# Regrouping the routed experts' passes in the last batch of a fused gated mixture-of-experts kernel

## The reference, cut to what matters

```python
s0, s1, s2 = (_dense(h, share_wi[i], share_wo[i]) for i in range(3))
out_a = relu(h @ expert_wi[type_idx]) @ expert_wo[type_idx]
out_b = relu(h @ expert_wi[type_idx + 1]) @ expert_wo[type_idx + 1]
expert_out = out_a * wa + out_b * wb
gi = concatenate([expert_out[:, 0], s0[:, 0], s1[:, 0], s2[:, 0]], axis=-1)
g = softmax(relu(gi @ gate_w1) @ gate_w2, axis=-1)
out = expert_out * g0 + s0 * g1 + s1 * g2 + s2 * g3
```

## Time and profile before

| | |
|---|---|
| median of 3 runs | 1036.35 us |
| the profiled execution's own time | 1037.89 us |
| its span, first to last instruction | 1035.9 us |
| TensorE matmul busy | 1029.4 us (99%) |
| TensorE weight load busy | 853.9 us (82%) |
| VectorE busy | 806.9 us (78%) |
| ScalarE busy | 415.5 us (40%) |
| granted TensorE clock | 1.000 |

### The profile page before, as it was taken

The page is one execution under the profiler, slowest core; times in us unless marked ns, Lnnn a source line. Parts: engine busy times, 40 slices in busy tenths (PEclk is TensorE's granted clock), DMA queues, the critical chain, the costliest instruction groups (busy, mean ns, idle before and its releaser), DMA issues.

```text
span 1035.9 us, 12766 instructions
## 1 busy us (share of the span) xinstructions
PE 1029.4 (99%) x4784; PEld 853.9 (82%) x4784; DVE 806.9 (78%) x1369; ACT 415.5 (40%) x695; POOL 16.4 (2%) x26
## 2 busy tenths in 40 slices
PE   9999999999999999999999999999999999999998
PEld 6688888888888888888888888888888888888898
DVE  6989977799767988489785997659976699745236
ACT  7654455533344234422434233442333423333232
POOL 1200000000000000000000000000000000000000
PEclk9999999999999999999999999999999999999999
DMA  6388999786454754465544664546645475456581
GB/s 214 123 294 287 299 366 373 291 303 236 152 203 153 264 193 163 162 235 204 208 166 159 242 234 146 196 164 245 215 149 203 163 258 201 142 191 216 200 323 74
DMA packets 38304, 223.02 MB, mean 215 GB/s; under 512 B 4515, under 2 KB 5283, under 8 KB 16611
## 3 DMA queue, kind: packets, MB, share of 16 engines
q1 hardware_dynamic: 35938, 209.63, 56.9%
q0 software_dynamic: 2304, 12.58, 3.2%
HBM read 188.51 MB, written 33.69 MB: 215 GB/s over the span
## 4 chain that ended last, share of the span: by engine, by line
PE 95%; DMA 2%; DVE 2%; issue 0%; ACT 0%; SPq 0%; DVEq 0%
PE ps_up L680 14%; PE ps_up L710 14%; PE ps_up L711 14%; PE ps_down L752 14%; PE ps_down L753 14%; PE ps_down L756 14%; PE ps_aux L673 2%; PE ps_aux L674 2%; PE ps_aux L675 2%; DMA wi<-split_wi 1%; DVE y L1691 1%; DMA wo<-split_wo 1%; PE ps_aux L853 1%; PE ps_aux L850 1%; PE ps_aux L849 1%; PE ps_aux L833 1%
## 5 line engine op out<-in xcount | busy, mean ns | idle before, releaser
L1081 ACT ACTIVATE hid_hi<-ps_up 128x512 fp32r<-128x512 f32 (+1 forms) x336 | 193.6, 576 | 494.2 <-PE ps_up L680 493.4
L1344 DVE SCALAR_TENSOR_TENSOR hid_lo<-ps_up,hid_hi 128x512 fp32r<-128x512 f32 (+1 forms) x336 | 219.8, 659 | 170.6 <-ACT hid_hi L1081 169.9
L710 PE MATMUL ps_up<-x_hi_all,wi 128*128 128x512 f32 (+1 forms) x660 | 250.3, 381 | 0.3 <-DMA wi<-split_wi 0.3
L711 PE MATMUL ps_up<-x_hi_all,wi 128*128 128x512 f32 (+1 forms) x660 | 249.9, 380 | 0.0
L752 PE MATMUL ps_down<-hid_hi,wo 128*128 128x512 f32 (+1 forms) x640 | 245.4, 384 | 0.2
L753 PE MATMUL ps_down<-hid_hi,wo 128*128 128x512 f32 (+1 forms) x640 | 245.1, 384 | 0.0
L680 PE MATMUL ps_up<-x_lo_all,wi 128*128 128x512 f32 (+1 forms) x660 | 197.3, 380 | 0.2 <-DVE x_lo_all L1335 0.2
L756 PE MATMUL ps_down<-hid_lo,wo 128*128 128x512 f32 (+1 forms) x640 | 193.7, 384 | 0.0
L710 PEld LDWEIGHTS ps_up<-x_hi_all,wi 128*128 128x128 f32 x660 | 124.1, 188 | 24.6 <-DMA wi<-split_wi 1.0
L711 PEld LDWEIGHTS ps_up<-x_hi_all,wi 128*128 128x128 f32 x660 | 124.1, 188 | 23.1
L680 PEld LDWEIGHTS ps_up<-x_lo_all,wi 128*128 128x128 f32 x660 | 122.0, 188 | 24.2 <-DVE x_lo_all L1335 0.4
(11 more groups left out here) (259 smaller groups left out, 898.0 us busy)
## 6 DMA issues: line engine op xcount, KB each, us to landing
wi<-split_wi SPq DMA_DIRECT2D x70, 1024.0 KB, 4.9
wo<-split_wo SPq DMA_DIRECT2D x70, 1024.0 KB, 4.9
modb<-mod_scratch SPq DMA_DIRECT2D x28, 512.0 KB, 5.9
split_wi<-wi SPq DMA_DIRECT2D x10, 1024.0 KB, 7.4
split_wo<-wo SPq DMA_DIRECT2D x10, 1024.0 KB, 8.0
xt<-in_x SPq DMA_DIRECT2D x8, 512.0 KB, 5.7
split_wi<-ex POOLq DMA_DIRECT2D x4, 1024.0 KB, 9.6
split_wo<-ex POOLq DMA_DIRECT2D x4, 1024.0 KB, 4.9
```

Of the source, the lines that this page charges most:

```text
L710: pe.matmul(ps, w_hi, x2_hi[:, parity, c, tokens], start=c == 0, stop=False)
L711: pe.matmul(ps, w_lo, x2_hi[:, parity, c, tokens], start=False, stop=False)
L1081: act.activation(hid_hi[:, k % NU, tokens], ps_up[k % NU][:, tokens], ACT.Relu).then_inc(hid_hi_ready, 1)
L1344: dve.scalar_tensor_tensor(hid_lo[:, k % NU, tokens], ps_up[k % NU][:, tokens], 0.0, f32(hid_hi[:, k % NU, tokens]), ALU.max, ALU.subtract ...
```

## The change: what it does

The first routed expert (ffn 3) runs on all 512 tokens in slots 24 to 31. The second (ffn 4) runs on tokens 0 to 127 in slots 32 to 39, into bank ps_aux1, and on tokens 128 to 511 in slots 40 to 47, into ps_down. There are 48 slots instead of 56, and no weights are loaded twice: the last unit of ffn 4 is loaded once into places of its own (`held_wi`, `held_wo`), where it stays for both passes. ScalarE reads ffn 3 out in slots 34 and 36, one c each. The gate starts at slot 40 as before. The first 128 tokens of ffn 4 are added to y, all four mixes run on full-width y (mix1 at 44.5, the others at 45.5), and at 47.5 ffn 4's later 384 tokens are added straight from ps_down. `store0` writes tokens 0 to 127, `store1` tokens 128 to 511.

```diff
 LAST_PLANS = {
-    "sync": {47: ["store0"], 55.5: ["store1"]}, "tensor": {41.5: ["gate_hidden"]}, "scalar": {43: ["gate_exp"]},
-    "vector": {40: ["gate_part"], 42: ["gate_logits"], 43.5: ["gate_soft", "final_scale"],
-               44.5: ["final_early0"], 45: ["final_early1"], 45.5: ["final_early2"], 46: ["final_early3"],
-               47.5: ["final_late0"], 48.5: ["final_late1"], 49.5: ["final_late2"], 50.5: ["final_expert_b"],
-               55.5: ["final_expert_a"]}, "gpsimd": {},
+    "sync": {47: ["store0"], 47.5: ["store1"]}, "tensor": {41.5: ["gate_hidden"]}, "scalar": {43: ["gate_exp"]},
+    "vector": {40: ["gate_part"], 42: ["gate_logits"], 43.5: ["gate_soft", "final_scale"], 44.5: ["mix1"],
+               45.5: ["mix2", "mix3", "mix0"], 47.5: ["final_expert_b"]}, "gpsimd": {},
 }
...
-LAST_PASSES = ((0, slice(0, T)), (1, slice(0, T)), (2, slice(0, T)), (3, slice(0, HALF)), (4, slice(0, HALF)),
-               (4, slice(HALF, T)), (3, slice(HALF, T)))
+FIRST = 128
+LAST_PASSES = (*((ffn, slice(0, T)) for ffn in range(FFNS - 1)), (FFNS - 1, slice(0, FIRST)), (FFNS - 1, slice(FIRST, T)))
 LAST_SLOTS = len(LAST_PASSES) * TPF
-AGAIN = LAST_SLOTS - TPF
+HELD = UNITS - 1
...
-        again_wi = [(xg_hi, xg_lo), (ct_hi[:, :, :], ct_lo[:, :, :])]
-        again_wo = [(wc_hi[:, 0:UT * E], wc_lo[:, 0:UT * E]),
-                    tuple(t[:, 0, :, :].rearrange("p c t -> p (c t)") for t in (x2_hi, x2_lo))]
+        held_wi = (xg_hi, xg_lo)
+        held_wo = (wc_hi[:, 0:UT * E], wc_lo[:, 0:UT * E])
...
-                if last and k in (33, 34):
-                    load_again_wi(k - 33)
-                if last and k in (35, 37):
-                    load_again_wo((k - 35) // 2)
-                if last and k >= SLOTS:
-                    return
-                if k % 4 == 0 and not (last and m + 1 >= UNITS) and unit_of(b, m + 1)[0] > 0:
+                if last and k == 23:
+                    load_held_wi()
+                if last and k == 27:
+                    load_held_wo()
+                if k % 4 == 0 and not (last and m + 1 >= HELD) and unit_of(b, m + 1)[0] > 0:
                     load_wo(b, m + 1)
-                if k % 4 == 2 and not (last and m + 2 >= UNITS) and unit_of(b, m + 2)[0] > 0:
+                if k % 4 == 2 and not (last and m + 2 >= HELD) and unit_of(b, m + 2)[0] > 0:
                     load_wi(b, m + 2)
...
                 elif step == "store0":
-                    sp.wait_ge(final_mixed[0], (NS + 1) * CT)
-                    sp.dma_start(out[f].rearrange("p (c t) -> p c t", c=CT)[:, :, half(0)], x2[:, p.f_parity, :, half(0)])\
+                    sp.wait_ge(mixed, f * 8 + 8)
+                    sp.dma_start(out[f].rearrange("p (c t) -> p c t", c=CT)[:, :, 0:FIRST], x2[:, p.f_parity, :, 0:FIRST])\
                         .then_inc(last_stored[0], 16)
                 elif step == "store1":
                     for c in range(CT):
-                        sp.wait_ge(final_mixed[1], (NS + 1) * CT + c + 1)
-                        sp.dma_start(out[f].rearrange("p (c t) -> p c t", c=CT)[:, c, half(1)], x2[:, p.f_parity, c, half(1)])\
+                        sp.wait_ge(final_mixed, c + 1)
+                        sp.dma_start(out[f].rearrange("p (c t) -> p c t", c=CT)[:, c, FIRST:T], x2[:, p.f_parity, c, FIRST:T])\
                             .then_inc(last_stored[1], 16)
...
-                    if k % TPF == 0 and ffn > 0 and at < SLOTS:
+                    if k % TPF == 0 and ffn > 0 and not (last and ffn == FFNS - 1 and at < SLOTS):
                         pe.wait_ge(y_ready, b * 8 + (2 * ffn - 1 + c))
...
-                    if SLOTS <= at < AGAIN:
-                        bank = ps_aux[1][:, c * HALF:(c + 1) * HALF]
+                    if last and ffn == FFNS - 1 and at < SLOTS:
+                        bank = ps_aux[1][:, c * FIRST:(c + 1) * FIRST]
...
             def mixture(b, k, parity, last):
-                if k % TPF == 0 and 0 < k < SLOTS:
+                if k % TPF == 0 and 0 < k < SLOTS and not (last and k // TPF == FFNS - 1):
                     read_out(b, k // TPF - 1, parity)
...
+                if last and k in (34, 36):
+                    read_out(b, NS, parity, (k // 2 - 17,))
...
-                else:
-                    at, h = int(step[-1]), int(step.startswith("final_late"))
-                    i = MIX_ORDER[at]
-                    if at == 0:
-                        dve.wait_ge(gate_soft, (B - 1) * 6 + 6)
-                    final_add(h, at, parity, lambda c: y[:, y_at(i, parity), c, half(h)], g[:, i:i + 1])
+                    for c in range(CT):
+                        if c == 0:
+                            dve.wait_ge(last_down, 1)
+                        else:
+                            dve.wait_ge(down_done, (B - 1) * SLOTS + LAST_SLOTS)
+                        dve.wait_ge(mixed, B * 8 - 1 + c)
+                        dve.scalar_tensor_tensor(x2[:, parity, c, FIRST:T], ps_down[c][:, FIRST:T], final_w[:, 1:2],
+                                                 x2[:, parity, c, FIRST:T], ALU.mult, ALU.add).then_inc(final_mixed, 1)
...
                     if final(f):
-                        add_expert_b(f, half(0), experts_ready)
+                        add_expert_b(f, slice(0, FIRST), lambda c: ps_aux[1][:, c * FIRST:(c + 1) * FIRST])
```

More of the change, by code:

```diff
@@ L136 @@
 GATING = {"gate_hidden", "gate_part_hi", "gate_part_lo", "gate_logits", "gate_exp", "gate_part", "gate_soft",
-          "mix0", "mix1", "mix2", "mix3", "store", "store0", "store1", "final_scale", "final_expert_a", "final_expert_b",
-          *(f"final_early{i}" for i in range(NS + 1)), *(f"final_late{i}" for i in range(NS))}
+          "mix0", "mix1", "mix2", "mix3", "store", "store0", "store1", "final_scale", "final_expert_b"}
 def later(count):
@@ L340, in build @@
         final_scale = sem("final_scale")
-        final_mixed = sems("final_mixed", 2)
-        again_loaded = sems("again_loaded", 2)
+        final_mixed = sem("final_mixed")
+        held_loaded = sems("held_loaded", 2)
         warm = sem("warm")
@@ L559, in load_wo, with load_held_wi, load_held_wo @@
                 sp.dma_start(f32(wo[:, buf, :, :]).rearrange("p s f -> p (s f)"), source).then_inc(wo_landed[buf], 16)
[L561 to L571, removed]
+            def load_held_wi():
+                source = split_wi[bass.ds(expert["now"] + FFNS - 1, 1), HELD % 2].rearrange("o p (s c f) -> (o p) s c f", s=2, c=CT)
+                for part, place in enumerate(held_wi):
+                    sp.dma_start(f32(place), source[:, part, :, :]).then_inc(held_loaded[0], 16)
+            def load_held_wo():
+                source = split_wo[bass.ds(expert["now"] + FFNS - 1, 1), HELD % 2].rearrange("o p (s f) -> (o p) s f", s=2)
+                for part, place in enumerate(held_wo):
+                    sp.dma_start(f32(place), source[:, part, :]).then_inc(held_loaded[1], 16)
             def load_x(m):
@@ L692, in up @@
                     pe.wait_ge(wi_ready, u + 1)
-                if j == 0 and b > 0 and at < SLOTS:
+                held = last and u == HELD
+                if j == 0 and b > 0 and at < SLOTS and not held:
                     pe.wait_ge(wi_landed[u % 2], 16 * ((b - 1) * (UNITS // 2) + u // 2 + 1))
-                if j == 0 and at >= AGAIN:
-                    pe.wait_ge(again_loaded[u % 2], 64)
+                if j == 0 and at < SLOTS and held:
+                    pe.wait_ge(held_loaded[0], 32)
                 ps = ps_up[at % NU][:, tokens]
                 def weights(c):
-                    if at >= AGAIN:
-                        return [w[:, c, j * P:(j + 1) * P] for w in again_wi[u % 2]]
+                    if held:
+                        return [w[:, c, j * P:(j + 1) * P] for w in held_wi]
                     cols = slice(c * UF + j * P, c * UF + (j + 1) * P)
@@ L726, in down @@
                     pe.wait_ge(wo_ready, u + 1)
-                if j == 0 and b > 0 and at < SLOTS:
+                held = last and u == HELD
+                if j == 0 and b > 0 and at < SLOTS and not held:
                     pe.wait_ge(wo_landed[u % 2], 16 * ((b - 1) * (UNITS // 2) + u // 2 + 1))
-                w_hi, w_lo = again_wo[u % 2] if at >= AGAIN else (wo_hi[:, u % 2, :], wo_lo[:, u % 2, :])
+                if j == 0 and at < SLOTS and held:
+                    pe.wait_ge(held_loaded[1], 32)
+                w_hi, w_lo = held_wo if held else (wo_hi[:, u % 2, :], wo_lo[:, u % 2, :])
                 pe.wait_ge(hid_hi_ready, b * SLOTS + (at + 1))
@@ L1081, in relu, with read_out @@
                 act.activation(hid_hi[:, k % NU, tokens], ps_up[k % NU][:, tokens], ACT.Relu).then_inc(hid_hi_ready, 1)
-            def read_out(b, ffn, parity):
+            def read_out(b, ffn, parity, tiles=range(CT)):
                 act.wait_ge(down_done, b * SLOTS + (ffn + 1) * TPF)
@@ L1090, in read_out @@
                     act.wait_ge(wa_ready, b + 1)
```

(15 more changed lines are left out.)

14 lines of the change are left out of this document (3 added, 11 removed).

## The result

The changed kernel takes 1040.44 us in the median (1039.71 to 1042.15, 6 runs), the kernel before, run beside it, 1035.89 us (1035.41 to 1036.43, 6 runs). The ratio is 1.0039, with an interval of 1.0026 to 1.0052: slower, by 4.55 us between the medians, where 4.4 was forecast.

A forecast was written before the change was run, and what follows sets the result against it. It took TensorE's matmul pace, set by weight loads in the narrow pass, then VectorE's closing additions as bounds. TensorE +0.5 us and the ending +3.9 made +4.4 on 1036.35: 1040.8 us, range 1038.3 to 1042.2.

The forecast's parts named there:

- Wide matmuls: TensorE's 512- and 384-token matmuls: 0.2267 and 0.1733 us each, columns at 2.4 GHz plus 0.0133 us.
- The narrow matmul: 128-token pass on TensorE: each matmul paced by its weight load at 0.111 us, 10.66 us for 96.
- Rival A: Narrow matmuls go by columns or near it, 0.0667 us each; total +0.1 us, 1036.5, not slower; chance 0.07.
- The Trainium skill's 81 ns: Documented pace for 128-column loads and matmuls: narrow pass 7.8 us, sum 2.9 us lower, 1037.9; 0.03 of 0.07 chance.
- Border waits: TensorE's waits at the borders of the short passes: 1.43 us before, zero after the change.
- The stretch: TensorE from ffn 3's first up matmul to the last up matmul's start: 48.92 us against 48.38, +0.5.
- VectorE's tail: From the last up matmul's start to the end, six mix additions delay the output: 9.74 us against 5.87, +3.9.
- finals: VectorE's last two additions, of the last expert: first starts 5.34 us after the last up matmul starts, end at 6.48.
- T: The start of TensorE's last up matmul, from which the end of the kernel is timed; 1030.03 us before the change.
- Rival B: The mixes do not decide, the last additions follow TensorE at 2.97 us; total +2.0 us, 1038.4; chance 0.05.
- rival C: Granted clock falls to 1.2 GHz in the narrow pass and stays through the 384-token pass: +15 us, 1056; chance 0.03.
- Outside the span: Execution time beyond the profiled span, 2.0 us before; the span's difference was applied unchanged to the median.

The follow-up runs named there:

- the 16-token run: The changed kernel with FIRST = 16 instead of 128, the late pass taking the other 496 tokens: 1053.25 us, ratio 1.0163.
- the one-mix run: The changed kernel with mix2, mix3 and mix0 left out of the last batch, only mix1 kept: 1038.16 us, ratio 1.0015.

## Why the prediction was right

Point by point:

- **Wide matmuls**: 0.227 and, at 384 columns, 0.173 us were both met (the last 384-token slot, 1027.12 to 1029.20, is 2.08 us). Columns at 2.4 GHz and 0.0133 on top held from 256 to 512.
- **The narrow matmul**, the term with the least behind it: 0.111 taken, 0.1117 measured. The nearest rows, 8-column matmuls in the opening, were the right measure, and the 16-token run shows why: no width below 128 makes it shorter. Rival A falls. The Trainium skill's 81 ns (TensorE: Matmul & The Clock Gate, section Back-to-back issue gap) is not met by any row here. Nor is the narrow pair at 0.120, the upper bound.
- **Border waits**: zero, as said. The stretch came out at +0.7 us for +0.5; the 0.17 between is not resolved into steps.
- **VectorE's tail**: finals at T + 5.34 and their end at T + 6.48, both to the hundredth; end of the span 3.2 us later for 3.26. One reading beside the sum was off: 18 matmuls follow T, not 15. The 15th is the last into the first of the two banks and lets the first final start; TensorE itself ends 3.46 us behind T (1032.49), not 2.97. VectorE is later than either, so the sum does not change. Rival B falls by the missing bracket, and the one-mix run shows what it would have been.
- **The clock**, rival C: it did not come in this kernel, but the argument against it was weak. The clock at 1.00 "where loads fill all the time" was seen with 256 columns. At 96 it fell. That it stayed at 128 is luck as far as that argument goes. The chance of 0.03 was given to a danger that lay 32 columns away, where it cost 5 us; at 64 and 16 tokens it cost 8.5 and 10.
- **Outside the span**: I carried 2.0 us over. All kernels of the changed form have 1.6 to 1.7 us between their time and their span (medians over 4 to 11 runs each), all of the kernel before's form 2.0. So +4.56 in the trace should be +4.2 in the time; the medians say +4.55, the ratio's interval 2.7 to 5.4. That the medians differ by the forecast to within 0.15 us is therefore in part luck.
- **What the prediction left out** is not a term but a cause. It said that the block of mixes stands behind the last low part, which is the order of the code. The runs show what is under it: reordered, the mixes free 2.1 us, and with the stretch shortened as well (256 tokens) they hang on the gate, which hangs on when the second expert's early part is done.

## What to carry to other kernels

A shorter pass pays on TensorE only while its columns outlast the weight load: by these rows that ends at some 240 columns ((0.1117 - 0.0133) x 2400, an estimate), and at 96 columns and below the clock went too. Where the whole output needs one value (here the gate), count the time from the piece of work that it hangs on to the end, against the length of the chain behind it (13.6 to 14.7 us here): a regrouping that brings that piece nearer to the end moves the bound from TensorE to the chain. And try first whether the waits can be had without the regrouping: exchanging two banks left the tail alone and made the traced stretch 1.4 us shorter, though half of that came from weights that landed sooner, and the medians can't tell it from nothing.

## What the runs showed of the hardware that was not expected

- The granted clock fell to 1.2 GHz under a stream of loads and matmuls without a gap, in the narrow pass with 16, 64 and 96 columns (window 1006 to 1010 with 96: matmuls busy for 4.00, loads for 3.96 of 4.00 us); with 128 in the same place it stayed at 1.00. It was down for 20.5, 17.1 and 10.2 us, on into the late pass.
- At 1.2 GHz a narrow pair took 0.21 us where it took 0.11 at 2.4 GHz: the load's pace goes with the clock too.
- The time outside the span is some 0.35 us shorter with programs of the changed form (medians of 1.6 to 1.7 us) than with those of the form before (2.0), in all runs. No run explains it.
